# L0's decays as product scans over rows that a DMA broadcasts, in place of exps of sums over R; one-hots, threshold counts and first gather placed anew

## What is computed

```python
xn = layernorm(x)
x = x + mamba_block_L0(xn) + leaf_tree_L0(xn)      # 8 heads of 64, state 16
xn = layernorm(x)
x = x + mamba2_L1(xn) + moe_L1(xn)                  # 4 heads of 128, state 64

# the recurrence of a mixer
dA = exp(dt * A)
def step(state, inp):
    dA_t, dBx_t = inp
    state = state * dA_t[:, :, None, None] + dBx_t
    return (state, state)
# y = states . C + D * x;  y = rmsnorm(y * silu(z)) @ W_out

# the experts: each of 8 takes its best 1024 of 4096 tokens
scores = softmax(xt @ Wr)
G, idx = top_k(scores.T, k)
h = gelu(X_in @ W1 + b1);  X_e = h @ W2 + b2
out = zeros.at[idx].add(G * X_e)
```

## Time and profile before

| | us |
|---|---|
| median of 3 runs | 1750.13 |
| lowest and highest | 1749.46, 1754.74 |
| the profiled execution, whole | 1762.29 |
| its span, first to last instruction | 1760.2 |
| mean granted TensorE clock, share of full | 0.935 |

### The profile page before, as it was taken

One profiled execution on the slowest core, in us unless ns is written; L12 is line 12 of the kernel. 1 busy time (PEld: TensorE's weight loads), 2 busy tenths in 40 slices (PEclk: granted clock), 3 DMA queues, 4 the chain that ended last, 5 costly groups with the idle time before them and its releaser, 6 DMA issues.

```text
span 1760.2 us, 23296 instructions
## 1 busy us (share of the span) xinstructions
PE 1582.4 (90%) x7307; PEld 1092.0 (62%) x7307; DVE 1120.2 (64%) x2583; ACT 768.2 (44%) x1562; POOL 710.1 (40%) x751
## 2 busy tenths in 40 slices
PE   4989999999999999998878889999868988898896
PEld 3555756557575756656534555555557877787886
DVE  4767586676858577672388888788745445545442
ACT  1435162533426162441245555666445444444452
POOL 1456456263645536364012222323324342434242
PEclk8979999999999999998978899999979999999998
DMA  6000100101010010101141111111023233423222
GB/s 193 1 12 13 38 24 1 60 0 48 12 48 12 0 60 0 36 13 37 37 134 34 57 37 57 60 61 60 28 79 91 64 71 69 94 61 70 70 43 24
DMA packets 66855, 84.00 MB, mean 48 GB/s; under 512 B 12360, under 2 KB 57296, under 8 KB 66768
## 3 DMA queue, kind: packets, MB, share of 16 engines
q1 hardware_dynamic: 54480, 65.86, 11.4%
q0 software_dynamic: 12288, 17.05, 5.8%
HBM read 57.53 MB, written 25.36 MB: 47 GB/s over the span
## 4 chain that ended last, share of the span: by engine, by line
PE 25%; issue 13%; POOL 6%; DVE 5%; ACT 2%; another core or an unknown queue 1%; POOLq 1%; DMA 0%; DVEq 0%; ACTq 0%; SPq 0%
PE bank L2065 24%; POOL yb L921 2%; POOL Xs L913 2%; POOL ry L929 1%; PE bank L2448 1%; DVE OL L1864 1%; DVE am L1879 1%; ACT m0big L1318 1%; DVE EW L2005 1%; POOL ry L926 0%; POOLq L967 0%; DVE w2l L2016 0%; POOL out L978 0%; DVE hits L1783 0%
## 5 line engine op out<-in xcount | busy, mean ns | idle before, releaser
L2020 DVE TENSOR_TENSOR aml<-m0big,amh 128x512 fp32r<-128x512 f32 x128 | 87.9, 691 | 228.2 <-ACT amh L1323 213.9
L1318 ACT ACTIVATE m0big<-bank,eb 128x512 f32<-128x512 f32 x128 | 87.7, 685 | 218.9 <-PE bank L2065 192.1
L978 POOL DMA_INDIRECT out<-EW,IDX x64 | 111.6, 1744 | 160.4 <-DVE EW L2005 143.6
L2065 PE MATMUL bank<-w2h,amh 128*128 128x256 f32 x512 | 152.7, 298 | 0.0
L2065 PE MATMUL bank<-w2h,aml 128*128 128x256 f32 x512 | 148.5, 290 | 0.0
L2065 PE MATMUL bank<-w2l,amh 128*128 128x256 f32 x512 | 148.4, 290 | 0.0
L2065 PE MATMUL bank<-h2T,EW 128*128 128x512 f32 x320 | 146.7, 595 | 0.3
L2065 PEld LDWEIGHTS bank<-Xdt,E 128*128 128x128 f32 x768 | 95.4, 200 | 55.9 <-issue 55.9
L952 POOL DMA_INDIRECT xg<-rows_d,IDX x64 | 62.4, 975 | 142.0 <-DVE IDX L1872 90.2
L2065 PE MATMUL bank<-EW,am 128*128 128x256 f32 x512 | 115.8, 379 | 1.2 <-DVE am L1642 1.2
L2065 PE MATMUL bank<-xTh,w1h 128*128 128x512 f32 x256 | 104.9, 410 | 9.0 <-ACT m0big L1318 7.6
(11 more groups left out here) (327 smaller groups left out, 3851.7 us busy)
## 6 DMA issues: line engine op xcount, KB each, us to landing
EW<-in_e_w SPq DMA_DIRECT2D x16, 1024.0 KB, 5.7
m0big<-dA_d SPq DMA_DIRECT2D x16, 512.0 KB, 4.7
xin<-in_L_attn_x SPq DMA_DIRECT2D x8, 512.0 KB
xp<-in_L_attn_x SPq DMA_DIRECT2D x8, 512.0 KB, 3.7
rows_d<-xo SPq DMA_DIRECT2D x8, 512.0 KB, 3.0
x_d<-xb SPq DMA_DIRECT2D x8, 512.0 KB, 4.0
xnT_d<-nT SPq DMA_DIRECT2D x8, 512.0 KB, 4.4
out<-x SPq DMA_DIRECT2D x32, 128.0 KB, 1.7
```

The source lines that it names most:

```text
L978: g.indirect_dma_start(out=out_rows, out_offset=bass.IndirectOffsetOnAxis(ap=IDX[:, 4 * u + c:4 * u + c + 1], axis=0), in_=ye[:, q, c, :], ...
L1318: a.activation(am2[:, j % 2, :], bank[j % 2][:, :], ACT.Gelu, bias=eb1[:, u // 2, j:j + 1]).then_inc(gelu_sig.sem, 1)
L2020: v.tensor_tensor(aml[:, j % 4, :], am2[:, j % 2, :], amh[:, j % 4, :], ALU.subtract).then_inc(am_low.sem, 1)
L2065: return t.matmul(out_, lhsT, rhs, start=first, stop=last)
```

## The change

- L0: `terms`, R, `decay_sums`, SEG's exps and Gm are gone. `decay_log_sums` moves into `head`, behind the in-projection, and also transposes the log decays to LOGT (32 rows, one for each chunk and head); `decay_exp` moves into ACT's `head` and also writes dAT0, their exps. SP stores dAT0 to HBM (`store_decays`) and loads each chunk's 1024 decays back, broadcast to all 128 partitions (`load_decays0`, 512 KB each, two buffers). DVE's `chunk` scans them into E, two scans of 512, behind `zs`; the mask products read GP out of PSUM. The products' signal M takes the place of Bs in PE's wait ahead of GP. The identity for the scans lies in b2. SP's loop over steps is written out.
- L1: the 15 counts are in the tiles c = 0, 1, 3 of steps 0 to 4; `above`, `prefixes`, `ranks`, `slots` go to tiles 22 to 25; the one-hots of expert 0 come 16 a tile in tiles 27 and 28.
- Border: `gather(0)` in tile 30, `tokens(0)` on PE ahead of the barrier, POOL no longer in it; ACT and DVE take the tokens ahead of the first weights.
- Experts: bunches of 16, four one-hots at each j of the even unit; on PE `slots(e, 0)` at j = 6 of the even unit, `slots(e, 1)` at j = 1 of the odd one; `index` at j = 3 of the odd unit, behind it both gathers of the next expert; POOL scatters before it gathers.

```diff
+    def store_decays(i):
+
+        sp.wait_ge(own, 2)
+        s0.dA.wait_ge(sp, i, 1)
+        for q in range(2):
+            s0.dA_loaded[q].wait_ge(sp, i, 0)
+        sp.dma_start(dA0_d.rearrange("c (h t) -> (c h) t", t=P), dAT0[:, :]).then_inc(s0.dA_stored.sem, 16)
+
+    def load_decays0(i, c):
+
+        if c >= 2:
+            s0.E.wait_ge(sp, i, 2 * (c - 1))
+        else:
+            s0.dA_stored.wait_ge(sp, i, 16)
+            s0.E.wait_ge(sp, i - 1, 2 * (c + 3))
+        sp.dma_start(dA0[c % 2][:, :], dA0_d[c].partition_broadcast(P)).then_inc(s0.dA_loaded[c % 2].sem, 16)
+
+    def decays_of(i):
+        store_decays(i)
+        load_decays0(i, 0)
+        load_decays0(i, 1)
+
+    def later_decays_of(i):
+        load_decays0(i, 2)
+        load_decays0(i, 3)
+
...
+    decays_of(0)
+    later_decays_of(0)
     load_x(2)
+    decays_of(1)
     load_residual(1)
+    later_decays_of(1)
     store_back(0)
-    with sp.Fori(1, STEPS - 2) as b:
+    for b in range(1, STEPS - 2):
         load_x(b + 2)
+        decays_of(b + 1)
         load_residual(b + 1)
+        later_decays_of(b + 1)
         store_back(b)
+    decays_of(STEPS - 1)
     load_residual(STEPS - 1)
+    later_decays_of(STEPS - 1)
...
-    gather(0)
+        if n + 2 == TILES1:
+            gather(0)
...
     y_rms1(STEPS - 1, CH - 1)
     gather(1)
-    pool.drain().then_inc(phase, 1)
-    pool.wait_ge(phase, 9)
...
     for u in range(UNITS):
-        if u % 2 == 0 and u:
+        if u:
             scatter(u - 1)
-        if u + 2 < UNITS:
+        if u % 2 and u + 1 < UNITS:
+            gather(u + 1)
             gather(u + 2)
-        if u % 2:
-            scatter(u - 1)
...
+        s.dA_stored.wait_ge(act, i, 0)
+        a.activation(dAT0[:, 1:P], LOGT[:, 1:P], ACT.Exp).then_inc(s.dA.sem, 1)
...
-        def decays(j):
-            s.seg_full.wait_ge(act, i, c * L.segs + j + 1)
-            a.activation(E[:, q, 512 * j:512 * (j + 1)], SEG[:, :], ACT.Exp).then_inc(s.E.sem, 1)
-
-        s.intra_full.wait_ge(act, i, c - 1)
-        decays(0)
...
         p = front_wait(act, L, s, i, f"xt{c}")
         s.xdt.wait_ge(act, i, c - 1)
         s.xd.wait_ge(act, i, c - 1)
         a.activation(Xsb[:, q, :], p[:, :], ACT.Copy).then_inc(s.xsb.sem, 1)
-        for j in range(1, L.segs):
-            decays(j)
...
+        s.dA_loaded[q].wait_ge(dve, i, 16 * (c // 2 + 1))
+        s.intra_full.wait_ge(dve, i, c - 1)
+        for j in range(L.segs):
+            v.tensor_tensor_scan(E[:, q, 512 * j:512 * (j + 1)], dA0[q][:, 512 * j:512 * (j + 1)], ID0, 0.0,
+                                 ALU.mult, ALU.add).then_inc(s.E.sem, 1)
...
         s.g_full.wait_ge(dve, i, c + 1)
-        if not L.tree:
-            threshold(i, c, ch)
-        v.tensor_tensor(Gm[:, q, :], GP, triU[:, :], ALU.mult).then_inc(s.gm.sem, 1)
         if c >= 2:
             front_wait(dve, L, s, i, f"state{c-2}")
         else:
             front_wait(dve, L, s, i - 1, f"state{c+2}")
         v.tensor_copy(Bs[:, q, 0:L.state], BTP[:, 0:L.state]).then_inc(s.bs.sem, 1)
         s.xsb.wait_ge(dve, i, c + 1)
-        s.intra_full.wait_ge(dve, i, c - 1)
         v.tensor_tensor(Xdt[:, q, :].rearrange("p (h e) -> p h e", h=nh),
                         Xsb[:, q, :].rearrange("p (h e) -> p h e", h=nh),
                         s.dtv_buf[:, 0, c * nh:(c + 1) * nh].unsqueeze(2).to_broadcast([P, nh, hp]),
                         ALU.mult).then_inc(s.xdt.sem, 1)
-        s.gm.wait_ge(dve, i, c + 1)
         for j in range(L.segs):
             s.E.wait_ge(dve, i, c * L.segs + j + 1)
             e3 = E[:, q, 512 * j:512 * (j + 1)].rearrange("p (h t) -> p h t", h=4)
-            v.tensor_tensor(e3, e3, Gm[:, q, :].unsqueeze(1).to_broadcast([P, 4, P]),
-                            ALU.mult).then_inc(s.M.sem, 1)
+            v.tensor_tensor(e3, e3, GP.unsqueeze(1).to_broadcast([P, 4, P]), ALU.mult).then_inc(s.M.sem, 1)
...
-    def onehots(e, b):
-
-        m = 3 * e + b
-        dve.wait_ge(iotas, 6)
-        if b != 1:
-            ol_used.wait_ge(dve, e, b // 2)
-        for k in range(BUNCH * b, min(BUNCH * (b + 1), TILES)):
-            ins = v.tensor_scalar(OL[:, m % 2, k % BUNCH, :], iotab[:, :], lof[:, e, k:k + 1], None,
-                                  ALU.is_equal)
-        ins.then_inc(ol_ready.sem, 1)
+    def onehot(e, k):
+
+        if k == 0:
+            dve.wait_ge(iotas, 6)
+        ins = v.tensor_scalar(OL[:, k // BUNCH, k % BUNCH, :], iotab[:, :], lof[:, e, k:k + 1], None,
+                              ALU.is_equal)
+        if k % BUNCH == BUNCH - 1:
+            ins.then_inc(ol_ready.sem, 1)
...
-        if n < 15:
-            threshold(n)
+        if c != 2 and i < 5:
+            threshold(3 * i + c - c // 3)
...
-        elif n == 18:
+        elif n == 22:
             above()
-        elif n == 19:
+        elif n == 23:
             prefixes()
-        elif n == 22:
+        elif n == 24:
             ranks()
-        elif n == 23:
+        elif n == 25:
             slots()
         elif n == 26:
             slot_parts()
             high_onehots(0)
-            onehots(0, 0)
         elif n in (27, 28):
-            onehots(0, n - 26)
+            for k in range(TILES // 2):
+                onehot(0, TILES // 2 * (n - 27) + k)
         elif n == 29:
             index(0)
...
                 if j == 0:
                     high_onehots(e + 1)
-                elif j < 7 and j % 2:
-                    onehots(e + 1, j // 2)
-                elif j == 7:
-                    index(e + 1)
+                for k in range(4):
+                    onehot(e + 1, 4 * j + k)
+            elif q and e + 1 < NE and j == 3:
+                index(e + 1)
...
     def decay_log_sums(L, s, i):

         s.a.wait_ge(pe, i, 1)
-        s.bs.wait_ge(pe, i, 0)
+        s.M.wait_ge(pe, i, 0)
         m = CH * L.heads
         for j, mat in enumerate((triU, strL, ones)):
-            last = mm(CUM[:, 32 * j:32 * j + m], mat[:, :], s.dtv_buf[:, 1, 0:m])
+            mm(CUM[:, 32 * j:32 * j + m], mat[:, :], s.dtv_buf[:, 1, 0:m])
+        last = t.transpose(LOGT, s.dtv_buf[:, 1, 0:m], ident[:, :])
...
-        def decay_sums(j):
-            s.E.wait_ge(pe, i, c * L.segs + j)
-            mm(SEG[:, :], strL[:, :], R[:, 512 * j:512 * (j + 1)]).then_inc(s.seg_full.sem, 1)
-
-        s.R.wait_ge(pe, i, c + 1)
-        decay_sums(0)
         if c == 0:
             s.xc.wait_ge(pe, i, 6)
         p = open_front(pe, L, s, i, f"xt{c}")
...
             last = t.transpose(p[:, cols(k)], s.u_buf[:, k, cols(c)], ident[:, :])
         filled(last, s, L, f"xt{c}")
         n = L.state
-        s.bs.wait_ge(pe, i, c)
+        s.M.wait_ge(pe, i, c * L.segs)
         if c == 0:
-            s.ex.wait_ge(pe, i, 1)
-        if not L.tree:
-
-            if isinstance(i, int) and i == 0 and c == 0:
-                pe.wait_ge(ph0, 2)
-            cnt_sig.wait_ge(pe, i, c)
-            mm(CNT, ones[:, :], cnt[:, :])
+            s.dA.wait_ge(pe, i, 1)
         mm(GP, s.u_buf[0:n, 4, cols(c)], s.Ct_buf[0:n, cols(c)])
         t.transpose(BTP[:, 0:n], s.u_buf[0:n, 4, cols(c)], ident[0:n, 0:n]).then_inc(s.g_full.sem, 1)
-        for j in range(1, L.segs):
-            decay_sums(j)
...
+    s1.t1.wait_ge(pe, STEPS, 0)
+    tokens(0)
+    pe.drain().then_inc(phase, 1)
+    pe.wait_ge(phase, 8)
...
-            if u % 2 == 0 and u + 2 < UNITS and j > 2 and j % 2:
-                slots(u // 2 + 1, (j - 3) // 2)
+            if u % 2 == 0 and u + 2 < UNITS and j == 6:
+                slots(u // 2 + 1, 0)
+            elif u % 2 and u + 1 < UNITS and j == 1:
+                slots(u // 2 + 1, 1)
```

More of the change, by code:

```diff
@@ L37 @@
 ROW = D + NE
-BUNCH = 11
+BUNCH = 16
 NH1 = 4
@@ L216, in program @@
         dts = sb("dts", [P, 8, CH * 8])
-        Gm = sb("Gm", [P, 2, P])
+        ex = sb("ex", [P, 3, CH * 8])
+        dtv = sb("dtv", [P, 3, CH * 8])
         mv = sb("mv", [P, CH, 2])
@@ L234, in program @@
         zs = sb("zs", [P, 2, DI])
-        R = sb("R", [P, 8 * P])
+        dA0b = sb("dA0b", [P, 8 * P])
+        dAT0 = sb("dAT0", [CH * 8, P])
         E = sb("E", [P, 2, 8 * P])
@@ L262, in program @@
         hits1 = hits[:, :, :].rearrange("p t e -> p (t e)")
-        L1T = [R[:, P * k:P * (k + 1)] for k in range(7)]
+        L1T = [dA0b[:, P * k:P * (k + 1)] for k in range(7)]
+        dA0 = (dA0a, dA0b)
         wq, wrT, lvT, woT = (am[:, k, :].rearrange("p (k n) -> p k n", k=KD) for k in range(4))
@@ L337, in program @@
         pool_prep = sem("pool_prep")
+        own = sem("identity_rows_ready")
         phase = sem("phase")
@@ L856, in step0 @@
                     back_rms(b, 0, CH - 1, poolb)
-                if f is not None:
-                    terms(L, s, f, 0, pool0)
                 if b is not None:
@@ L1718, in step0 @@
                     dveb.end()
+            v.tensor_copy(ID0.rearrange("p (h t) -> p h t", h=4),
```

(40 more changed lines are left out.)

44 lines of the change are left out of this document (17 added, 27 removed).

## The result

The changed kernel takes 1761.1 us (median of four runs, 1760.2 to 1762.7), the kernel before beside it 1750.1: 1.0053 of it, 95% interval 1.0037 to 1.0070. It is slower by 11 us where the forecast said 30 us faster, and lies above the whole range. Measured a second time, the pair gave 1760.7 against 1750.6, 1.0055 (1.0036 to 1.0074).

The account below looks back on a forecast made before the run. PE is busiest; in L0 its queue nearly ties with DVE's chain with POOL, elsewhere PE waits and loses clock. Experts -46, border -9, L1 -14, L0 +39 sum to -30: 1720 us against the median 1750.1, range 1682 to 1744.

Parts of the forecast that it names:

- Experts, -46: Experts: PE's seven waits for one-hots OL, 30.6 us, go, with the half-clock stretches behind them: -46 us.
- The third rival: Experts: the next expert's gathers come too late, 4.4 us plus 2.2 for the clock, seven times: 1766 us, chance 0.08.
- Border, -9: Between L1 and experts: earlier gather(0), tokens turned before the barrier, transposes near 1281 instead of 1290.4 us: -9 us.
- L0, the sum on VectorE, +2: Steady L0 step, four chunks: scans +9.1, collisions +5.9, zs +1.5, less mask products, waits and old collisions: about +2 us.
- PE waits about 3.7 us before the transposes of chunk 2 [...] I take 3: Steady L0 step: this wait brings half clock, costing 3 us; a step loses 5 us, seven of them +35.
- L0, the first step, +4: First L0 step: scans +9.1, masks -8, fewer collisions -3, first rows perhaps late: +4 us, bounds 0 and +8.
- The rule on the ramp: L0: skill's clock ramp under one per cent of span, capping seven clock falls at 17.6 us instead of 21.
- three counts [...] 46 us [...] stay near 1.5 us without a fall of the clock: L1: PE's 4.09 us wait shrinks, a three-count step takes 46 us: -14 us, bounds -8 (48.3 a step) and -18.
- cover is DVE's slack there, at most 2 us if gone: L1: moving ranks, slots and the rest four tiles on costs nothing, at most 2 us.
- Rivals 1, 2 and 4: L0: 1, short wait or clock stands, 1699, 0.27; 2, PE's saving realized, 1667, 0.12; 4, rows late, 1748, 0.05.
- The range: Whole kernel: from 1682 us (L0 at +1) to 1744 us (L0 at +63).

Follow-up runs that it names:

- the second profile: The kernel before, profiled again without an edit: 1751.9 us, span 1749.8.
- awake_l0: Changed kernel plus six useless products a step on PE where it waits in L0: 1709.5 us, where the kernel before took 1763.1.
- awake_first: Changed kernel with useless products in L0 only at the first of PE's two waits: 1725.2 us, 0.9841 of the kernel before.
- counts_012: Changed kernel with L1's counts in tiles c = 0, 1, 2 and slots in tile 26: 1758.0 us, 1.0032 of the kernel before.

## Why the prediction was wrong

- **Experts, -46.** Right: -44.0 against the second profile. OL's waits are gone. The third rival didn't come: PE waits 0.7 us for rows in all.
- **Border, -9.** Right: -10.1.
- **L0, the sum on VectorE, +2.** Right in its busy part, wrong in its waits. Of the +1.9 the busy terms are +2.4 and the waits -0.5. VectorE's busy time rose by 1.7 us. Its waits for PE and ScalarE, which the forecast let go (-2.0), rose instead, from 2.2 to 7.3 us, 3.60 and 1.72 us of it behind the slow PE. Collisions with POOL cost 4.2 us a step (scans 0.8 twice and 0.2, Xdt 0.7 twice, two am 1.0), where I took 5.9. The exclusive lock that the Trainium skill states (SBUF — State Buffer, "SBUF: two separate sides") would make it 8.3 by the forecast's estimate, if all eight operations of POOL met one of VectorE at that port. The trace doesn't bear whole lengths out even where they met: in chunk 0 VectorE lost 1.5 us beside 2.1 us of POOL's work, and POOL's Xs took 1.96 us instead of 1.04, so both were held.
- **L0, "PE waits about 3.7 us before the transposes of chunk 2 [...] I take 3".** This is the step that failed, in the place, the number and the price of the waits. Before the transposes of chunk 2 PE doesn't wait at all. It waits in two places ahead of them, 3.7 us at chunk 1, which I had not looked at, and 2.4 us at y_turned(1). That 3.7 us stands in the forecast and in the trace is chance (the forecast's own terms, 12.8 less 8.9, give 3.9). VectorE's 12.8 us between the two mixed0 came as 13.24 us (508.99 to 522.23); the 8.9 us of PE beside it, from y_turned(1) to y_turned(2), became 14.65 us, because the clock had fallen by then. Half clock follows both waits; each lasts 10 us and costs 5, where I had one at 3 us, from stretches of 4.4 and 8 us elsewhere. A step cost 8 us instead of 5. awake_l0 shows it: with the waits filled, L0 gives back 42 of its 62 us, and awake_first that each wait brings a fall of its own. At chunk 1 the chain is the plainest in the kernel: two scans, Xdt, two mask products and am stand between zs of chunk 0 and zs of chunk 1, 7.5 us, and PE has 4.1 us of work beside them (475.58 to 479.72).
- **L0, the first step, +4.** Near by luck: it cost 4.9 us, but the terms named (+9.1, -8, -3) add up to -2, and the late rows that were to make up the difference didn't come.
- **The rule on the ramp.** I named it as a cap of 17.6 us, one per cent of the span, though the sum kept the uncapped 21. Filling the waits of L0 alone gave 45 us of span, 2.6%. The Trainium skill states the one per cent in TensorE: Matmul & The Clock Gate under "What's actually happening" (the prediction names the section next to it), for the start of a kernel. The section "HAM oscillation — how this bites in real kernels" of that page of the Trainium skill is the one that fits: a loop whose waits bring the clock down on every pass, and a cost of half the slowed time. The trace agrees with that one, 10 us at half clock costing 5.
- **L1, "three counts [...] 46 us [...] stay near 1.5 us without a fall of the clock".** Failed: the wait is 2.50 us, the clock falls, and a step takes 48.0 us, as by the forecast's lower bound. The link between them was right: in counts_012 the two steps with waits of 1.67 and 1.75 us and no fall take 46 us. The sum priced a count by the step's length and thought the place free. "cover is DVE's slack there, at most 2 us if gone" failed too: with slots in tile 25 a wait of 2.25 us and its half clock came, and the last part of L1 is 4.9 us longer.
- **Rivals 1, 2 and 4.** The clock did fall, and PE's saving was not realized (rival 2's 1667 also leaves out the +4 of the first step). No scan of L0 waited for its decay rows; their loads landed in about 4 us:

```profile
dA0a<-dA_d SPq DMA_DIRECT2D x16, 512.0 KB, 3.8
dA0b<-dA_d SPq DMA_DIRECT2D x16, 512.0 KB, 4.1
```

- **The range.** Its upper end held L0 at +63, which came; it did not hold that L1's gain would fail at the same time. 1744 and L1's 14.5 us make 1759.
